# A six-layer local-attention stack: squares in halves, head scaling ahead of the score maximum, rotary tables scaled two steps earlier, and the value projection two units at a time in high and low parts

## The chip, the cores and the metric

The kernel runs on 1 core of one Trainium2 chip. The metric is the device time of one execution in microseconds. TensorE, VectorE, ScalarE and GpSimd each work through a queue of their own in program order; SyncE's queue issues the DMAs. They meet only at semaphores. In the rows below they are called PE, DVE, ACT, POOL and SPq.

## The reference, cut to what matters

The program is one decoder layer of three parts (a Mamba block with a mixture of experts, a cross attention, and a stack of six local-attention layers), each followed by a residual sum and a layer norm. All of the change that takes time lies in the third part, the stack. It runs over 2 batches of 512 tokens with 128 features, and each of its six layers does:

```python
def attn_layer(x, Wqkv, qs, ksc, Wo):          # 16 heads of 64, window 32
    q, k, v = split(x @ Wqkv, 3)
    q = l2norm(q) * qs
    k = l2norm(k) * ksc
    q = q * cos * scale + rotate_half(q) * sin * scale
    k = k * cos * inv   + rotate_half(k) * sin * inv
    sim = einsum(q, k of this window and the one before) * 8.0, masked
    out = softmax(sim) @ v
    return out @ Wo
for i in range(6):
    x = attn_layer(shift_tokens(x), ...) + x
    x = ffn_layer(shift_tokens(x), ...) + x     # layer norm, gated GELU, 341 wide
```

## The kernel before, in words

`build_stack` (line 1083) writes the stack out by hand as a software pipeline. A layer is a `turn`; a turn has 16 steps `t`, one for each *unit* (a pair of heads of one batch; units 0 to 7 belong to batch 0, units 8 to 15 to batch 1), so the stack has 96 units. In step `t` the five queues work on different units at once:

- TensorE: the scores of unit t+1 (`scores`, L1307), the projection of "head unit" h = t+4 into two PSUM banks (`project`, L1266 to L1270; q for even h, k for odd h, six matmuls of 512 columns in high and low fp32r parts), the transposes of the probabilities (L1319), the output projection of unit t-1 (L1341), the value projection of unit t+1 (`project_v`, L1290: four fp32 matmuls of 128 columns, which the trace shows as eight passes), the mask for the next scores, the sums of squares over a head (`head_norm`, L1278), and the values times the probabilities (L1331).
- ScalarE: the squares of the projection, both banks in one instruction (`square`, L1426), the exponential of the scores (L1489), the copies out of PSUM (L1457, L1466, L1450), and from the sum of squares the logarithm and the root (L1433, L1437).
- VectorE: the maximum of the scores of unit t+1 (L1610) and its subtraction (L1616); `normalise_heads` for head unit t+3 (L1556, writes `st_turned`); `rotate` for head unit t+4, which multiplies the projection by the sine and the cosine table (L1545, L1546); then the row sums (L1640) and their reciprocals (L1644).
- GpSimd: the sum of the two halves of squares (L1673); the two additions that end the rotation (L1677, L1678); the probabilities divided by their sum (L1685); in half of the steps the low part of a weight (L1662).
- SyncE: the DMAs that place the turned heads for the scores (four for a q unit, eight for a k unit), and two that shift the copied values (`shift_values`).

Head unit h is projected and rotated in step h-4 and scaled by `normalise_heads` in step h-3. That instruction waits for both of GpSimd's additions. `rotate` reads the PSUM banks, and the next `project` waits for both products, since there is one pair of banks. In the rows below the names of tiles that share memory are those of the first owner: `h` is the tile of squares, `x` the sine product or the copied output, `mo_w` the cosine product or the scaled probabilities.

In steps 0 to 3 and 8 to 11 of a turn the feed-forward layer of a batch runs in between, as `stage` 0 to 3. Stage 0: `residual1` on VectorE (L1564), then the mean on TensorE (L1345), `centre` on VectorE (L1580), the square on ScalarE (L1501) and the variance on TensorE (L1349), which stands ahead of the next step's scores. Stage 1 scales the centred rows and starts the gates, stage 2 multiplies gate and value on VectorE (`gated`), and the value projection there waits for that. Stage 3 ends with `down` on TensorE, `residual2` on VectorE (L1571), and where a new layer follows the high part of the stream on ScalarE (L1518), for which the next projection waits. In step 11 and step 12 of each turn but the last, `scale_table` (L1444, two instructions of 1024 elements) writes the rotary tables of the next layer; it stands at the step's end, ahead of L1518. In the first turn there is no feed-forward layer in steps 0 to 3, so stage 0 occurs 11 times beside steps 0 to 15, and once more behind them.

From step 7 to 14 VectorE writes one eighth of the next layer's q and k weights as fp32r (`high_weights`, L1536), and GpSimd its rest (`low_weights`, L1662).

## Time and profile before

| | us |
|---|---|
| median of 3 runs | 1337.75 (1335.63 to 1342.5) |
| the profiled execution | 1334.07 |
| its span | 1332.3 |
| TensorE busy in the span | 1143.7 (86%) |
| VectorE, ScalarE, GpSimd busy | 951.0, 834.3, 671.2 |

The span is what the profiler saw between the first and the last instruction; 1.8 us of the profiled execution's time lie around it. Busy time adds up instructions and says nothing of what waits for what. TensorE's granted clock was 0.99 to 1.00 of full speed (2.4 GHz) in every stretch of 130 or 140 us from 470 to 1160 us; the stack runs from before 437.75 us to about 1319 us. One turn, from the scores of step 8 at 632.83 us to those of the next turn's step 8 at 781.05 us, took 148.2 us.

### The profile page before, as it was taken

The numbers are of one execution on the slowest core, as the hardware profiler recorded it, in microseconds if no ns is written. First come the engines' busy times: TensorE is split into PE (matmuls) and PEld (weight loads), VectorE is DVE, ScalarE is ACT, GpSimd is POOL, SyncE is SP. The second block draws the span as 40 slices with busy tenths as digits, with TensorE's granted clock in tenths as the row PEclk, the third lists the DMA queues.
The fourth block names the chain that finished last, engine by engine and source line by source line (L and its number), as shares of the span: only waits on it lengthen the run. The fifth ranks groups of instructions, "written<-read, shape, count | busy, mean of one in ns | idle before, by whom it ended". The sixth has DMA issues, their size and how long they took to land. (4 is left out here: it accounts for less than half of the span.)

```text
span 1332.3 us, 25833 instructions
## 1 busy us (share of the span) xinstructions
PE 1143.7 (86%) x9541; PEld 716.3 (54%) x9636; DVE 951.0 (71%) x1207; ACT 834.3 (63%) x1260; POOL 671.2 (50%) x522
## 2 busy tenths in 40 slices
PE   7787879998656898998988998899989989899975
PEld 2222347776224665656555655656555655566541
DVE  2798957776646787877877787867877786877733
ACT  4553446665354667776776767676767667676834
POOL 1555524443326665755655465755555555645510
PEclk9888969999878999999999999999999999999987
DMA  3000035100203443445334442444333532434310
GB/s 108 1 0 0 1 49 198 48 24 1 95 1 79 128 111 77 108 103 132 80 92 105 116 111 72 110 115 121 78 92 102 134 96 69 108 91 110 87 46 16
DMA packets 75507, 107.08 MB, mean 80 GB/s; under 512 B 25347, under 2 KB 31938, under 8 KB 75002
## 3 DMA queue, kind: packets, MB, share of 16 engines
q1 hardware_dynamic: 75386, 105.47, 30.3%
q8 instruction: 76, 1.25, 0.4%
q14 instruction: 45, 0.37, 0.1%
HBM read 30.89 MB, written 0.59 MB: 24 GB/s over the span
## 5 line engine op out<-in xcount | busy, mean ns | idle before, releaser
L1673 POOL TENSOR_TENSOR st_sq_sum<-h 128x512 f32<-128x512 f32 x96 | 130.1, 1355 | 201.4 <-ACT h L1426 201.4
L1677 POOL TENSOR_TENSOR mo_w<-mo_w,x 128x512 f32<-128x512 f32 x96 | 122.3, 1274 | 154.0 <-DVE mo_w L1546 154.0
L1426 ACT ACTIVATE h<-banks 128x1024 f32<-128x1024 f32 x96 | 98.3, 1024 | 144.1 <-PE banks L1270 143.8
L1610 DVE TENSOR_REDUCE st_mx<-banks 128x8 f32<-128x512 f32 x96 | 66.4, 692 | 165.6 <-PE banks L1307 165.2
L1278 PE MATMUL banks<-st_sq_sum,head_ones 128*128 128x512 f32 x192 | 106.6, 637 | 47.9 <-POOL st_sq_sum L1673 46.6
L1556 DVE SCALAR_TENSOR_TENSOR st_turned<-st_rn,mo_w 128x1024 f32<-128x1024 f32 x96 | 124.3, 1295 | 5.9 <-POOL mo_w L1678 5.5
L1545 DVE TENSOR_TENSOR x<-banks,st_scaled 128x1024 f32<-128x1024 f32 x96 | 117.0, 1218 | 15.4 <-ACT h L1426 14.0
L1290 PEld LDWEIGHTS banks<-st_wv,stream 128*128 128x128 f32 x768 | 100.7, 192 | 49.7 <-issue 49.3
L1678 POOL TENSOR_TENSOR mo_w<-mo_w,x 128x512 f32<-128x512 f32 x96 | 122.5, 1276 | 0.0
L1307 PE MATMUL banks<-st_k_blocks,st_qT 128*32 128x128 f32 x3072 | 105.5, 279 | 16.9 <-DMA st_k_blocks<-st_turned 16.9
L1331 PEld LDWEIGHTS banks<-st_p_blocks,st_vs 128*64 128x64 f32 x1536 | 77.8, 137 | 74.2 <-issue 72.9
L1546 DVE TENSOR_TENSOR mo_w<-banks,st_scaled 128x1024 f32<-128x1024 f32 x96 | 116.4, 1213 | 0.0
L1457 ACT ACTIVATE st_p_blocks<-banks 64x512 f32<-64x512 f32 x192 | 112.3, 585 | 3.5 <-PE banks L1319 1.1
L430 POOL TENSOR_TENSOR ma_dbx<-ma_u,ma_b_rows 128x1024 f32<-128x1024 f32 x32 | 75.4, 2360 | 76.1 <-ACT ma_b_rows L288 51.9
L1266 PE MATMUL banks<-st_y_high,st_w_high 128*128 128x512 f32 x192 | 91.9, 479 | 21.2 <-issue 11.6
L1685 POOL TENSOR_TENSOR mo_w<-st_prob,st_ri 128x512 f32<-128x512 f32 x96 | 100.3, 1045 | 17.9 <-DVE st_ri L1644 17.9
L1290 PE MATMUL banks<-st_wv,stream 128*128 128x128 f32 x768 | 102.4, 277 | 0.8 <-issue 0.8
L1433 ACT ACTIVATE st_rn<-banks,fill 128x512 f32<-128x512 f32 x96 | 66.0, 688 | 58.9 <-PE banks L1278 58.9
L1341 PE MATMUL banks<-x,st_wo 128*128 128x512 f32 x192 | 101.7, 612 | 0.9 <-ACT x L1450 0.8
L1331 PE MATMUL banks<-st_p_blocks,st_vs 128*64 128x64 f32 x1536 | 99.4, 228 | 2.8 <-ACT st_p_blocks L1457 2.1
L1307 PEld LDWEIGHTS banks<-st_k_blocks,st_qT 128*32 128x32 f32 x3072 | 79.1, 111 | 41.5 <-DMA st_k_blocks<-st_turned 23.1
L1331 PE MATMUL banks<-st_p_blocks,st_vn 128*64 128x64 f32 x1536 | 94.8, 222 | 0.0
(230 smaller groups left out, 2629.2 us busy)
## 6 DMA issues: line engine op xcount, KB each, us to landing
st_qT<-st_turned SPq DMA_DIRECT2D x192, 128.0 KB, 2.4
st_k_blocks<-st_turned SPq DMA_DIRECT2D x384, 64.0 KB, 2.0
st_vs<-st_vn SPq DMA_DIRECT2D x96, 192.0 KB, 2.5
st_w_raw<-in_w_qk SPq DMA_DIRECT2D x12, 512.0 KB, 4.7
st_vs<-st_vn SPq DMA_DIRECT2D x96, 48.0 KB, 2.1
mo_w_all<-gate_rows SPq DMA_DIRECT2D x1, 3072.0 KB, 12.9
st_wv<-in_w_v SPq DMA_DIRECT2D x12, 256.0 KB, 3.0
st_wo<-in_wo SPq DMA_DIRECT2D x12, 256.0 KB, 3.1
```

The lines of the kernel that those rows point to most:

```text
L1278: mm(NORM_BANK, C["head_ones"], sq_sum[:], start=True, stop=True).then_inc(norm_done.sem, 1)
L1290: last = mm(V_BANK[:, rows], Y[:, b, rows], wv[:, pair, :], start=True, stop=True)
L1307: last = mm(SCORE_BANK[rows].rearrange("p (o h i k) -> p o h i k", o=2, h=2, i=2)[:, odd, :, i, :], qT[:, r, pair, t0:t0 + WIN], k_blocks[ ...
L1331: last = mm(TURN_BANK[rows, P * j:P * j + P].rearrange("p (h o q) -> p h o q", h=2, q=WIN)[:, :, odd, :], (vn if odd else vs)[:, r, j, row ...
L1341: mm(OUT_BANK[b], wo[:, pair, :], oT[:, n % 2, :], start=(pair == 0), stop=(pair == 7)).then_inc(wo_step.sem, 1)
L1457: A(p_blocks[rows, r, half, :], TURN_BANK[rows, :], ACT.Copy).then_inc(pt_copied.sem, 1)
L1545: v.tensor_tensor(sin_part[:], QK_BANKS, scaled[:, which, 1], ALU.mult).then_inc(product_done.sem, 1)
L1546: v.tensor_tensor(cos_part[:, which], QK_BANKS, scaled[:, which, 0], ALU.mult).then_inc(product_done.sem, 1)
L1556: v.scalar_tensor_tensor(turned[:, h % 4], rn[:, h % 2, :].unsqueeze(1).to_broadcast([P, 2, SEQ]), 1e12, cos_part[:, which], ALU.min, ALU. ...
L1673: nc.gpsimd.tensor_tensor(sq_sum[:], sq[:, 0, :], sq[:, 1, :], ALU.add).then_inc(sq_summed.sem, 1)
L1677: nc.gpsimd.tensor_tensor(cos_part[:, which, 0, :], cos_part[:, which, 0, :], sin_part[:, 1, :], ALU.subtract).then_inc(add_done.sem, 1)
L1678: nc.gpsimd.tensor_tensor(cos_part[:, which, 1, :], cos_part[:, which, 1, :], sin_part[:, 0, :], ALU.add).then_inc(add_done.sem, 1)
```

## The change

It has four parts, all in `build_stack`:

1. `square` writes two instructions of 512 elements, each behind its own half of the projection; `project` counts `qk_done` after each half.
2. `normalise_heads(t + 3)` moves on VectorE's queue from behind the score's maximum, subtraction and `residual1` to the very start of the step.
3. `scale_table` moves on ScalarE's queue from the end of steps 11 and 12 to their start.
4. The value projection works on two units' columns at once: 256 columns of weights and two of the four row tiles in each step, as three fp32r matmuls (high by high, high by low, low by high) for each tile. It and the copy run one step ahead (unit t+2); the shifting DMAs are issued every other step with twice the bytes. The weights of V get a high part on VectorE and a low part on GpSimd, four more of each per layer, in steps 8, 10, 12 and 14.

To make room, `gate`, `act` and `xn` move into tiles that are free by then (`cr_onehot`, `cr_line` and `cr_bias` in the rows of the new order).

```diff
 def square(s, h):
-            ac.wait_ge(*qk_done.at(s.turn, h + 1))
             if sq_summed.any(s.turn, h):
                 ac.wait_ge(*sq_summed.at(s.turn, h))
-            A(sq[:], QK_BANKS, ACT.Square).then_inc(sq_done.sem, 1)
+            for part in range(2):
+                ac.wait_ge(*qk_done.at(s.turn, 2 * h + part + 1))
+                A(sq[:, part, :], ps[:, part, :], ACT.Square).then_inc(sq_done.sem, 1)
...
 # ScalarE, body
+                if t in (11, 12) and not s.last:
+                    ac.wait_ge(*product_done.at(s.turn, 2 * (t + 4)))
+                    scale_table(s, t - 11, 1)
                 if stage == 1:
...
-                if t in (11, 12) and not s.last:
-                    ac.wait_ge(*product_done.at(s.turn, 2 * (t + 4)))
-                    scale_table(s, t - 11, 1)
                 if s.resplit(job, stage):
...
 # VectorE, body
                 n = t + 1
+                if t >= -3 and s.unit(t + 3):
+                    normalise_heads(s, t + 3)
                 if t >= -1 and s.unit(n):
...
                 if stage == 0:
                     residual1(s, job)
-                if t >= -3 and s.unit(t + 3):
-                    normalise_heads(s, t + 3)
...
 # VectorE, high_weights
             v.tensor_copy(w_high[:, i, :], w_raw[:, i, :]).then_inc(w_high_done.sem, 1)
+            if i % 2 == 1:
+                g = i // 2
+                dv.wait_ge(*places.wv_in.at(s.turn, 16 * ahead + 16))
+                if ahead:
+                    dv.wait_ge(*v_done.at(s.turn, 10 + 2 * g))
+                v.tensor_copy(wv_high[:, g, :], wv_raw[:, g, :]).then_inc(w_high_done.sem, 1)
...
 # TensorE, project_v
-            pe.wait_ge(*wv_in[pair // 4].at(s.turn, 16 * (n // 16) + 16))
-            for tile in range(4):
-                rows = slice(P * tile, P * tile + P)
-                last = mm(V_BANK[:, rows], Y[:, b, rows], wv[:, pair, :], start=True, stop=True)
+            if n % 16 < 8 and half == 0:
+                pe.wait_ge(*w_split.at(s.turn, SPLITS * (n // 16) + v_split(g)))
+            if n % 8 == 0:
+                pe.wait_ge(*y_low_done.at(s.turn, n // 8 + 1))
+            for i in range(2):
+                rows = slice(P * (2 * half + i), P * (2 * half + i) + P)
+                out = V_BANK[:, 2 * P * i:2 * P * i + 2 * P]
+                mm(out, y_high[:, b, rows], wv_high[:, g, :], start=True, stop=False)
+                mm(out, y_high[:, b, rows], wv_low[:, g, :], start=False, stop=False)
+                last = mm(out, y_low[:, b, rows], wv_high[:, g, :], start=False, stop=True)
...
-                if t >= -1 and s.unit(t + 1):
-                    project_v(s, t + 1, job, stage)
+                if t >= -2 and s.unit(t + 2):
+                    project_v(s, t + 2, job, stage)
```

How the order moves on VectorE, around a step without feed-forward work and one of stage 0 (step 0 of the second turn). Before:

```order
L1610 TENSOR_REDUCE st_mx<-banks 128x8
L1616 TENSOR_TENSOR st_prob<-banks,st_mx 128x512
L1564 TENSOR_TENSOR stream<-banks,stream 64x512 x2
L1556 SCALAR_TENSOR_TENSOR st_turned<-st_rn,mo_w 128x1024
L1580 TENSOR_TENSOR st_dx<-stream,banks 128x512
L1545 TENSOR_TENSOR x<-banks,st_scaled 128x1024
L1546 TENSOR_TENSOR mo_w<-banks,st_scaled 128x1024
L1640 TENSOR_REDUCE st_rs<-st_prob 128x8
```

The same place now, behind the reciprocal of the step before:

```order
L1574 SCALAR_TENSOR_TENSOR st_turned<-st_rn,mo_w 128x1024
L1630 TENSOR_REDUCE st_mx<-banks 128x8
L1636 TENSOR_TENSOR st_prob<-banks,st_mx 128x512
L1582 TENSOR_TENSOR stream<-banks,stream 64x512 x2
L1598 TENSOR_TENSOR st_dx<-stream,banks 128x512
L1563 TENSOR_TENSOR x<-banks,st_scaled 128x1024
L1564 TENSOR_TENSOR mo_w<-banks,st_scaled 128x1024
L1658 TENSOR_REDUCE st_rs<-st_prob 128x8
```

The rows are one step of stage 0; a regular step reads the same without the residual (64x512 x2) and without `st_dx`. The head scaling went from the third place to the first; maximum, subtraction and residual now stand behind it, and nothing is left between residual and centring.

On ScalarE, from the table load that ends step 10 to the stream's high part that ends step 11. Before:

```order
L1511 ACT_TABLE_LOAD
L1426 ACTIVATE h<-banks 128x1024
L1489 ACTIVATE st_prob<-st_prob 128x512
L1457 ACTIVATE st_p_blocks<-banks 64x512 x2
L1466 ACTIVATE st_vn<-banks 128x512
L1433 ACTIVATE st_rn<-banks,fill 128x512
L1437 ACTIVATE st_rn<-st_rn,fill 128x512
L1450 ACTIVATE x<-banks 128x512
L1444 ACTIVATE st_scaled<-st_table,st_rope_scale 128x2x512 x2
L1518 ACTIVATE st_y_high<-stream 128x512
```

Now:

```order
L1526 ACT_TABLE_LOAD
L1455 ACTIVATE st_scaled<-st_table,st_rope_scale 128x2x512 x2
L1437 ACTIVATE h<-banks 128x512 x2
L1504 ACTIVATE st_prob<-st_prob 128x512
L1468 ACTIVATE st_p_blocks<-banks 64x512 x2
L1478 ACTIVATE st_vn<-banks 128x512
L1444 ACTIVATE st_rn<-banks,fill 128x512
L1448 ACTIVATE st_rn<-st_rn,fill 128x512
L1461 ACTIVATE x<-banks 128x512
L1530 ACTIVATE st_y_high<-stream 128x512
```

The scaled tables went from ahead of the stream's high part to ahead of the squares, which are two instructions now; between them the order is the same.

## Rows read from the trace of the kernel before

**Rows 1.** The page: the span, and each engine's busy time.

```profile
span 1332.3 us, 25833 instructions
PE 1143.7 (86%) x9541; PEld 716.3 (54%) x9636; DVE 951.0 (71%) x1207; ACT 834.3 (63%) x1260; POOL 671.2 (50%) x522
```

**Rows 2.** The page, costliest groups: busy, mean ns of one | idle before, releaser.

```profile
L1278 PE MATMUL banks<-st_sq_sum,head_ones 128*128 128x512 f32 x192 | 106.6, 637 | 47.9 <-POOL st_sq_sum L1673 46.6
...
L1307 PE MATMUL banks<-st_k_blocks,st_qT 128*32 128x128 f32 x3072 | 105.5, 279 | 16.9 <-DMA st_k_blocks<-st_turned 16.9
```

**Rows 3.** Timeline, 700 to 712 us, a regular step: start, duration, engine, line, [idle before].

```profile
702.33 1.08 PE L1307 MATMUL banks<-st_k_blocks,st_qT 128*32 128x128 f32 x32 [1.50 <-DMA st_k_blocks<-st_turned]
...
703.48 0.69 DVE L1610 TENSOR_REDUCE st_mx<-banks 128x8 f32<-128x512 f32 x1 [2.95 <-PE banks L1307]
...
703.92 0.40 PE L1270 MATMUL banks<-st_y_low,st_w_high 128*128 128x512 f32 x1
...
704.16 0.40 PE L1266 MATMUL banks<-st_y_high,st_w_high 128*128 128x512 f32 x1
...
704.81 1.22 DVE L1556 SCALAR_TENSOR_TENSOR st_turned<-st_rn,mo_w 128x1024 f32<-128x1024 f32 x1
...
705.05 1.02 ACT L1426 ACTIVATE h<-banks 128x1024 f32<-128x1024 f32 x1 [3.34 <-PE banks L1270]
...
706.11 1.22 DVE L1545 TENSOR_TENSOR x<-banks,st_scaled 128x1024 f32<-128x1024 f32 x1
706.15 1.05 PE L1290 MATMUL banks<-st_wv,stream 128*128 128x128 f32 x8
...
707.25 1.22 DVE L1546 TENSOR_TENSOR mo_w<-banks,st_scaled 128x1024 f32<-128x1024 f32 x1
...
707.49 1.12 PE L1278 MATMUL banks<-st_sq_sum,head_ones 128*128 128x512 f32 x2 [0.28 <-POOL st_sq_sum L1673]
...
708.55 1.27 POOL L1677 TENSOR_TENSOR mo_w<-mo_w,x 128x512 f32<-128x512 f32 x1 [1.11 <-DVE mo_w L1546]
...
709.63 1.08 PE L1307 MATMUL banks<-st_k_blocks,st_qT 128*32 128x128 f32 x32
...
711.02 1.04 POOL L1685 TENSOR_TENSOR mo_w<-st_prob,st_ri 128x512 f32<-128x512 f32 x1
```

**Rows 4.** Timeline, 545 to 549 us, VectorE and GpSimd.

```profile
546.08 2.05 DVE L1556 SCALAR_TENSOR_TENSOR st_turned<-st_rn,mo_w 128x1024 f32<-128x1024 f32 x1 [0.29 <-POOL mo_w L1678]
...
546.00 1.04 POOL L1685 TENSOR_TENSOR mo_w<-st_prob,st_ri 128x512 f32<-128x512 f32 x1
```

**Rows 5.** Timeline, 712 to 721 us, a step of stage 0.

```profile
712.11 1.40 DVE L1564 TENSOR_TENSOR stream<-banks,stream 64x512 f32<-64x512 f32 x2
...
713.56 1.12 PE L1345 MATMUL banks<-stream,mean_ones 128*128 128x512 f32 x2
...
715.95 1.12 PE L1278 MATMUL banks<-st_sq_sum,head_ones 128*128 128x512 f32 x2 [0.37 <-POOL st_sq_sum L1673]
...
718.46 0.61 ACT L1501 ACTIVATE st_dsq<-st_dx 128x512 f32<-128x512 f32 x1
...
720.18 1.08 PE L1307 MATMUL banks<-st_k_blocks,st_qT 128*32 128x128 f32 x32
```

**Rows 6.** Timeline, 667 to 678 us, step 11 of a turn and what follows.

```profile
667.33 1.02 ACT L1426 ACTIVATE h<-banks 128x1024 f32<-128x1024 f32 x1
...
673.50 1.53 DVE L1571 SCALAR_TENSOR_TENSOR stream<-banks,st_ffn_param,stream 64x512 f32<-64x512 f32 x2 [1.93 <-PE banks L1376]
...
675.08 2.17 ACT L1444 ACTIVATE st_scaled<-st_table,st_rope_scale 128x1024 f32<-128x1024 f32 x2
...
677.16 0.62 ACT L1518 ACTIVATE st_y_high<-stream 128x512 fp32r<-128x512 f32 x1
```

**Rows 7.** Groups by line and form: the casts of q and k weights on VectorE.

```profile
L1536 DVE CAST st_w_high<-st_w_raw 128x256 fp32r<-128x256 f32 x48 | 33.5, 699 | 0.0
```

**Rows 8.** Timeline, 659 us, stage 2: the weight loads of the value projection.

```profile
659.20 0.97 PEld L1290 LDWEIGHTS banks<-st_wv,stream 128*128 128x128 f32 x8 [0.97 <-issue]
```

More of the change, by code:

```diff
@@ L1280, in project_v @@
         def project_v(s, n, job, stage):
-            b, pair = n // 8 % 2, n % 8
+            b, g, half = n // 8 % 2, n % 8 // 2, n % 2
             if v_copied.any(s.turn, n):
@@ L1329, in values @@
                         rows = slice(64 * head, 64 * head + 64)
+                        cols = slice(P * r + 64 * head, P * r + 64 * head + 64)
                         at = P * (2 * odd + head) + WIN * j
                         last = mm(TURN_BANK[rows, P * j:P * j + P].rearrange("p (h o q) -> p h o q", h=2, q=WIN)[:, :, odd, :],
-                                  (vn if odd else vs)[:, r, j, rows], p_blocks[:, r, :, at:at + WIN],
+                                  (vn if odd else vs)[:, q, j, cols], p_blocks[:, r, :, at:at + WIN],
                                   start=True, stop=True)
@@ L1356, in up_gate @@
             if j == 1:
-                pe.wait_ge(*v_copied.at(s.turn, min(t + 2, UNITS) if s.last else t + 2))
+                pe.wait_ge(*v_copied.at(s.turn, min(t + 3, UNITS) if s.last else t + 3))
             if j == 2:
@@ L1367, in up_value @@
             else:
-                pe.wait_ge(*v_copied.at(s.turn, min(t + 1, UNITS) if s.last else t + 1))
+                pe.wait_ge(*v_copied.at(s.turn, min(t + 2, UNITS) if s.last else t + 2))
                 pe.wait_ge(*act_done.at(s.turn, 3 * job + 2))
@@ L1596, in gated @@
                 dv.wait_ge(*w2_step.at(s.turn, 3 * job))
[L1597 removed]
+            v.scalar_tensor_tensor(act[0:rows, j, :], (OUT_BANK[job % 2] if j == 0 else V_BANK)[0:rows, :], ffn_param[0:rows, 2 + j:3 + j], gate[j % 2][0:rows, :],
                                    ALU.add, ALU.mult).then_inc(act_done.sem, 1)
@@ L1802, in program @@
         with ExitStack() as part:
-            spare = (x[:], h1[:], x1[:], weights.all[:].rearrange("p e g c -> p (e g) c"))
+            spare = (x[:], h1[:], x1[:], weights.all[:].rearrange("p e g c -> p (e g) c"), cross.place["bias"][:].rearrange("p t h k -> p t (h k)"),
+                     (cross.onehot[:, 0:SEQ], cross.line[:, 0:SEQ]))
             build_stack(nc, part, Y, stack, spare, d, C)
```

110 lines of the change are left out of this document (57 added, 53 removed).

## The prediction

> **What bounds the kernel now.** I read the page first. TensorE is busy 86% of the span and nothing else is over 71% [rows 1], which looks like a TensorE bound, but the list of groups shows what stands ahead of its instructions: 47.9 us of idle time before the head sums (they wait for GpSimd's sum of squares) and 16.9 us before the scores (they wait for the DMAs that place k) [rows 2]. These two waits are what the change is aimed at, so the question is what takes their place. For that I went to the timeline of one regular step [rows 3]. It runs from the scores at 702.33 us to those at 709.63 us, 7.30 us, and two chains hardly leave each other room in it. One is TensorE's queue, with 0.28 us of waiting. The other goes through three engines: the second product of the rotation ends at 707.25 + 1.22 = 708.47; GpSimd adds from 708.55 on and is free for the probabilities at 711.02, so the additions end about 2.55 us behind the products; the head scaling needs them. Before the change that scaling (704.81) comes behind the maximum (703.48) and the subtraction, when the additions are long done. Take from this: the additions end 1.4 us *behind* the start of the scores (711.02 against 709.63), while the maximum could start 1.15 us behind it (703.48 against 702.33).
>
> **Part 2, the order on VectorE.** I begin with this because it decides. VectorE now stands at the head scaling until the additions are done, and maximum, subtraction and the next rotation stand behind it. That closes a loop with nothing parallel in it: rotation, additions, scaling, maximum, subtraction, rotation. Its length from the rows: 2.55 to the end of the additions [rows 3], then the scaling starts 0.08 us behind GpSimd's probabilities [rows 4], maximum and subtraction take 1.33 (703.48 to 704.81), the rotation 2.36 (706.11 to 708.47) [rows 3]. The scaling itself has two prices in the trace: 1.22 alone [rows 3], and 2.05 in the one place where it had waited for the additions [rows 4]. There GpSimd's probabilities had started 0.08 us earlier, ran 1.04, and VectorE's instruction ended 1.22 - 0.13 behind them: it stood still until they were done. After the change this is the normal case, since GpSimd's probabilities follow the additions at once in its queue. So I take 2.05. Sum: 2.55 + 0.08 + 2.05 + 1.33 + 2.36 = 8.37; successive starts on VectorE overlap the end before by up to 0.1, so 8.3 us. With 1.22 it is 7.5 us.
>
> The Trainium skill (SBUF — State Buffer, "two separate sides") says that a VectorE instruction with two SBUF inputs and a GpSimd one that reads SBUF exclude each other on a shared port pair, and that whichever starts first has it to its end. The trace agrees in the row with 2.05. By that rule alone the 0.08 us decide: were the scaling first, the loop would be the 7.5 us one, and it is a rival below.
>
> Regular steps, without feed-forward work and not directly behind `residual2`, are 96 - 44 - 11 = 41. Each goes from 7.3 to 8.3: +41 us. The loop hides the DMA waits: the scaling of k ends earlier by more than the 1.50 us of the longest shown wait, so the 16.9 us go [rows 2, 3]. Net **+24**; with 7.5 us steps it would be 8 - 17 = -9.
>
> Stage 0, 11 times. The mean needs `residual1`, which needs the loop's first half. From the end of the products: 2.63 + 2.05 + 1.33 = 6.0, residual 1.40, 0.05 to the mean: 7.46. From the mean to the head sums 2.39 less the 0.37 waited there, less 0.15 for the cheaper value projection: 1.87. Head sums to the centred square 2.51, that to the next scores 1.72 [rows 5]. Sum 13.56. Before: 708.47 to 720.18, 11.71 [rows 3, 5]. +1.85 x 11 = **+20**; with a scaling of 1.22, +1.0 x 11 = 11. The head scaling used to fill VectorE's wait for the mean; now it stands empty.
>
> **Part 1, squares in halves.** Two instructions of 512 (0.61 for such a square [rows 5]) for one of 1.02 [rows 3]; the first is hidden under the second half of the projection, so the rotation could start some 0.4 us earlier. That removes head-sum waits only where TensorE is the bound. In the 41 regular steps the loop of part 2 does not contain the squares, so nothing is gained. Upper end if it did: the whole 47.9 us [rows 2]. In stages 1 and 2 some of it stays.
>
> **Part 3, tables early.** In step 11 the squares start at 667.33 with no idle time shown: ScalarE comes from a table load and is late already [rows 6]. Putting 2.17 us of tables there delays squares, sum of squares, head sums, `down` and `residual2` by 2.17 + 0.17. What comes back: the high part of the stream started at 677.16 and `residual2` had ended at 675.03 [rows 6], so up to 2.1 us. But behind it VectorE has to scale, find the maximum, subtract, cast twice and rotate before the next products, so I count 1.1 back, between 0 and 2.1. +1.25 x 5 turns = **+6** (ends +1 and +12).
>
> **Part 4, V in parts.** TensorE: six passes of 256 columns. A pass of 512 fp32r columns follows the last after 0.24 (703.92, 704.16), so 0.12 x 6 = 0.72 against 1.05 for the eight now [rows 3]; with a tail I take 0.15 saved, bounds 0 and 0.33. Over 96 units that could be 14 us, up to 32, if TensorE were the bound; I credit it only in stage 0, above, since elsewhere it turns into waiting. VectorE: 20 more casts of 0.70 [rows 7], 14 us if all lay in the loop, none if all fell into idle time; most of their steps are stage steps, so **+3**. Their low parts lie on GpSimd behind the probabilities, in time in which it waits. Fewer, larger shift DMAs free SyncE's queue, which is no longer what is waited for: nothing.
>
> **Stages 1 and 2.** Stage 2's value projection waits already for VectorE's gate products (0.97 us of idle time before its weights [rows 8]), and these stand behind a scaling that is 0.83 longer: +9 over 11 times. Against it stand the head-sum waits of stage 1, some 0.4 each, and 0.15 for V: -6. **+3**, ends -10 and +15.
>
> **Sum:** 24 + 20 + 6 + 3 + 3 = +56 on the profiled execution's 1334.1 us: **1390 us**. The median of the three runs stands 3.7 us above that execution, which is inside their spread.
>
> **The rivals.**
> *A, no stretch* (0.14). The scaling starts ahead of GpSimd's probabilities, or the pair at [rows 4] is a special case. For it: nearly all scalings before took 1.22, and 0.08 us is little. Against: both wait for the same additions, one of them in the queue right behind. Then -9 + 11 + 6 + 3 - 3 = +8: 1342 us, within 0.5% or just outside.
> *B, TensorE stays the bound* (0.10), the faster side. The place is the top of the step: if the additions end before the scores do, the scaling runs in time in which VectorE is idle (2.95 us ahead of the maximum at 703.48 [rows 3]) and delays nothing. It decides from the point where additions plus scaling (2.55 + 1.3 behind the products) end by 1.15 us behind the scores' start; now they would end 2.7 behind it. Squares in halves give back 0.4 of the missing 1.5, stretched DMA waits in odd steps the rest at times. Price: most of 47.9 and 16.9, and 14 for V, less 20 in stages 0 and the tables: about -45, 1290 us.
> *C, it costs more* (0.12). The low parts of V's weights and q's and k's (half of the steps) push GpSimd's sum of squares behind the maximum, casts then stand behind that sum as the scaling stands behind the probabilities, and stages 1 and 2 lose 1 to 2 us each: +20 more, 1410 us.
> That the change doesn't do what it says is excluded by the order of the new kernel's queues: the scaling does stand first.
>
> **How the numbers follow.** A measurement of this kernel tells about 0.5% (6.7 us) from no change. The forecast has 0.64, C 0.12, A 0.14, B 0.10. Slower by over 0.5%: the forecast, C and a third of A, 0.81. Within 0.5%: most of A, 0.09. Faster: B, 0.10. The range goes from below A (1342 less some 12 us of V that TensorE does give back) to C: 1330 to 1408, leaving out B and half of C.
>
> **What would show it.** Right: the idle time of VectorE moves from the maximum to the head scaling and names GpSimd's L1678 of before as its releaser; the mean duration of the scaling goes from near 1.22 to near 2; regular steps take 8.3 us and are even, without DMA waits; stage 0 grows by about 2 us; the transposes of the probabilities or the mean gain idle time on TensorE. Step by step wrong: a scaling of 1.22 us (A); regular steps under 7.3 us with the head sums' wait gone (B); squares of step 11 not later (part 3). If TensorE's idle time in the stack shrinks in total, the theory falls.

## The result and the profile after

| | before | after |
|---|---|---|
| median, 4 runs each on the same chip | 1336.69 us | 1402.14 us (1397.64 to 1406.66) |
| ratio, 95% interval | | 1.0483 (1.0448 to 1.0518) |
| the profiled execution | 1334.07 | 1398.13 |
| its span | 1332.3 | 1395.4 |

The change costs 65 us, 4.8%. The forecast was 1390 us, with a range of 1330 to 1408.

The page of the changed kernel, first its span and busy times, then the groups that answer to [rows 2] and the group of the head scaling:

```profile
span 1395.4 us, 25510 instructions
...
PE 1156.6 (83%) x9444; PEld 702.3 (50%) x9444; DVE 1009.8 (72%) x1231; ACT 851.8 (61%) x1356; POOL 707.7 (51%) x546
...
L1574 DVE SCALAR_TENSOR_TENSOR st_turned<-st_rn,mo_w 128x1024 f32<-128x1024 f32 x96 | 184.1, 1917 | 157.8 <-POOL mo_w L1700 149.0
...
L1281 PE MATMUL banks<-st_sq_sum,head_ones 128*128 128x512 f32 x192 | 110.3, 658 | 38.4 <-POOL st_sq_sum L1695 37.8
...
L1316 PE MATMUL banks<-st_k_blocks,st_qT 128*32 128x128 f32 x3072 | 105.5, 279 | 5.6 <-DMA st_k_blocks<-st_turned 5.6
```

TensorE's share fell from 86% to 83%. Of the two waits at which the change aims, the one for k's DMAs shrank, from 16.9 to 5.6 us. The head sums' seems to have fallen too, from 47.9 to 38.4 us, but the 47.9 us of [rows 2] are not all idle time. The mask's matmul stands right ahead of the head sums in TensorE's queue, and 95 of its 96 records are missing from the trace of the kernel before, so that its time reads as idle there. The trace of b3 below, whose edit leaves these instructions alone, has all of them. First the mask's matmuls before, then those of b3 and b3's head sums:

```profile
L1296 PE MATMUL banks<-mask,ident x1: 379/379/379, 417.1 to 417.1; 128*128 128x512 bf16 x1
...
L1296 PE MATMUL banks<-mask,ident x96: 379/379/650, 411.6 to 1273.6; 128*128 128x512 bf16 x96
...
L1278 PE MATMUL banks<-st_sq_sum,head_ones 128*128 128x512 f32 x192 | 108.8, 649 | 29.8 <-POOL st_sq_sum L1673 27.2
```

Against 29.8 us the head sums of the changed kernel wait longer, not shorter. With the mask left out of both traces it is 48.1 us before and 64.3 after. So 11 us of waits for DMAs are gone, and against them stand 158 us in which VectorE waits ahead of the head scaling, and a scaling that takes 1917 ns on average. Before, it took 1295 ns on average over the same 96. VectorE's wait costs time only where TensorE waits for VectorE in turn. Where that is, the waits list of the stack shows (engine, line, what it waited for: us in total, times, longest):

```profile
DVE st_turned L1574 <- POOL mo_w L1700: 131.1, 73, 1.8
...
PE banks L1355 <- DVE stream L1582: 28.2, 12, 2.6
...
PE banks L1281 <- POOL st_sq_sum L1695: 24.1, 31, 2.2
...
PE banks L1328 <- POOL mo_w L1707: 18.4, 25, 1.4
...
PE banks L1341 <- ACT st_p_blocks L1468: 14.7, 24, 1.9
...
PE banks L1297 <- DVE cr_bias L1615: 13.0, 17, 2.1
```

TensorE's waits are now spread over the whole step: for the residual ahead of the mean, for GpSimd's probabilities ahead of their transposes, for the copied probabilities, for the gates. No single one of them looks like the cause. I read them as places where TensorE meets a loop on the other engines that has become longer than its own work; the runs below test that.

**A regular step after the change.** The timeline from one step's scores to the next's, to be read beside [rows 3]:

```profile
643.48 1.08 PE L1316 MATMUL banks<-st_k_blocks,st_qT 128*32 128x128 f32 x32
...
644.07 1.29 POOL L1700 TENSOR_TENSOR mo_w<-mo_w,x 128x512 f32<-128x512 f32 x1
...
645.32 1.04 POOL L1707 TENSOR_TENSOR mo_w<-st_prob,st_ri 128x512 f32<-128x512 f32 x1
645.39 2.05 DVE L1574 SCALAR_TENSOR_TENSOR st_turned<-st_rn,mo_w 128x1024 f32<-128x1024 f32 x1 [1.80 <-POOL mo_w L1700]
...
647.36 0.68 DVE L1630 TENSOR_REDUCE st_mx<-banks 128x8 f32<-128x512 f32 x1
...
648.88 1.22 DVE L1563 TENSOR_TENSOR x<-banks,st_scaled 128x1024 f32<-128x1024 f32 x1
...
650.01 1.22 DVE L1564 TENSOR_TENSOR mo_w<-banks,st_scaled 128x1024 f32<-128x1024 f32 x1
...
651.31 1.28 POOL L1699 TENSOR_TENSOR mo_w<-mo_w,x 128x512 f32<-128x512 f32 x1 [2.73 <-DVE mo_w L1564]
...
651.75 1.08 PE L1316 MATMUL banks<-st_k_blocks,st_qT 128*32 128x128 f32 x32
```

651.75 - 643.48 = 8.27 us; the forecast was 8.3. The scaling waits 1.80 us, starts 0.07 us behind GpSimd's probabilities, stands still for as long as these run, and takes 2.05 us, as in [rows 4]. The maximum follows at 647.36, although its scores were there since about 644.6.

**A step of stage 0**, which answers to [rows 5]:

```profile
657.13 1.40 DVE L1582 TENSOR_TENSOR stream<-banks,stream 64x512 f32<-64x512 f32 x2
...
658.59 1.13 PE L1355 MATMUL banks<-stream,mean_ones 128*128 128x512 f32 x2 [2.56 <-DVE stream L1582]
...
659.75 0.69 DVE L1598 TENSOR_TENSOR st_dx<-stream,banks 128x512 f32<-128x512 f32 x1 [0.69 <-PE banks L1355]
...
660.50 1.02 PE L1281 MATMUL banks<-st_sq_sum,head_ones 128*128 128x512 f32 x2
...
662.91 0.61 ACT L1516 ACTIVATE st_dsq<-st_dx 128x512 f32<-128x512 f32 x1
...
664.63 0.65 PE L1316 MATMUL banks<-st_k_blocks,st_qT 128*32 128x128 f32 x16
```

From 651.75 to 664.63 it is 12.88 us (10.55 before). TensorE stands for 2.56 us in front of the mean, and VectorE for 0.69 us behind it with nothing to do.

**Step 11**, which answers to [rows 6]:

```profile
688.96 1.28 ACT L1526 ACT_TABLE_LOAD   x1
...
690.25 2.19 ACT L1455 ACTIVATE st_scaled<-st_table,st_rope_scale 128x1024 f32<-128x1024 f32 x2
...
692.35 1.06 ACT L1437 ACTIVATE h<-banks 128x512 f32<-128x512 f32 x2
...
694.81 1.97 PE L1281 MATMUL banks<-st_sq_sum,head_ones 128*128 128x512 f32 x2 [2.19 <-POOL st_sq_sum L1695]
...
700.25 1.53 DVE L1589 SCALAR_TENSOR_TENSOR stream<-banks,st_ffn_param,stream 64x512 f32<-64x512 f32 x2 [3.62 <-PE banks L1386]
...
701.83 0.62 ACT L1530 ACTIVATE st_y_high<-stream 128x512 fp32r<-128x512 f32 x1
```

The tables stand ahead of the squares, and the head sums wait 2.19 us. (They have moved from the end of their step to its start, not by two steps as the title has it.) What comes next costs again: the two head sums take 1.97 us where they take 1.02 in the stage 0 step above. The table of windows over the same place (window, length, busy time and count of PE, PEld, DVE, ACT, POOL, then PEclk, DMA share, GB/s):

```profile
690.00:694.80 4.80, 2.23 (x11) 1.09 (x9) 2.65 (x5) 4.76 (x8) 1.65 (x2) 1.00 0.50 111
694.80:698.00 3.20, 3.19 (x4) 1.41 (x5) 1.79 (x3) 1.96 (x4) 2.12 (x2) 0.52 0.37 99
```

Behind the wait the granted clock is 0.52, all but the lower of TensorE's two levels (1.2 GHz), for 3.2 us. Step 11 went from 11.17 us to 14.7 to 15.0 in four turns. In the first turn the wait is the same, 2.18 us, but the clock stays at 1.00 behind it, and the step takes 13.3 us: 2.1 more, which is the wait alone. So the low clock adds 1.4 to 1.7 us where it comes, and it does not come behind every such wait. The longer wait of stage 0, 2.56 us, shows the same. The next three rows are the stretches behind the wait of step 11 in the first turn, behind that of step 8 in the first turn, and behind that of the stage 0 step above:

```profile
535.70:538.70 3.00, 3.00 (x7) 1.44 (x8) 1.78 (x3) 2.21 (x4) 1.94 (x2) 1.00 0.34 87
500.40:503.40 3.00, 3.00 (x10) 1.89 (x8) 1.64 (x3) 0.27 (x2) 0.00 (x0) 0.50 0.39 92
658.60:661.60 3.00, 3.00 (x15) 1.69 (x17) 2.31 (x5) 1.02 (x3) 0.00 (x0) 1.00 0.40 96
```

Step 8 of the first turn takes 14.51 us, the others up to the last turn 12.88. Two of the eleven stage 0 steps have the low clock. The kernel before has such stretches too: each of its five steps 12 with tables has a wait of 2.32 us ahead of the projection; in four of them (10.9 to 11.2 us) the clock falls, in the fifth (10.56) it does not. What decides whether the clock falls behind a wait of this length is open.

**Where the time went.** I took the distance from one step's scores to the next in both traces, from step 3 of the first turn to the last scores of the stack (before 839.2 us, after 899.5), and summed the differences by kind of step, in us:

| steps | number | difference |
|---|---|---|
| stage 0 (0 and 8) | 11 | +25.7 |
| stages 1 and 2 (1, 2, 9, 10) | 22 | +7.5 |
| 3 | 6 | 0.0 |
| stage 3, tables in all turns but the last (11) | 6 | +16.9 |
| 12 | 6 | -18.0 |
| 4 to 7 | 24 | +10.3 |
| 13 to 15 | 16 | +17.9 |
| sum | 91 | +60.3 |

The rest of the 63.1 us between the spans lies ahead of step 3 (+3.9) and behind the last scores (-1.1). The rows mix the parts of the change; which part a difference belongs to only the runs below can tell.

### The profile page after: what moved, and what is told of

Same layout as the page of the kernel before. It is cut to its first block and busy times, and to the rows that moved or that the text cites. A ratio compares the mean times of both kernels' runs of the same rounds, so it can differ in the third digit from the quotient of the medians.

```text
span 1395.4 us, 25510 instructions
## 1 busy us (share of the span) xinstructions
PE 1156.6 (83%) x9444; PEld 702.3 (50%) x9444; DVE 1009.8 (72%) x1231; ACT 851.8 (61%) x1356; POOL 707.7 (51%) x546
## 5 line engine op out<-in xcount | busy, mean ns | idle before, releaser
L1574 DVE SCALAR_TENSOR_TENSOR st_turned<-st_rn,mo_w 128x1024 f32<-128x1024 f32 x96 | 184.1, 1917 | 157.8 <-POOL mo_w L1700 149.0
L1437 ACT ACTIVATE h<-banks 128x512 f32<-128x512 f32 x192 | 111.6, 595 | 86.0 <-PE banks L1273 83.4
L1281 PE MATMUL banks<-st_sq_sum,head_ones 128*128 128x512 f32 x192 | 110.3, 658 | 38.4 <-POOL st_sq_sum L1695 37.8
L1504 ACT ACTIVATE st_prob<-st_prob 128x512 f32<-128x512 f32 x96 | 60.5, 630 | 110.2 <-DVE st_prob L1636 110.2
L1341 PEld LDWEIGHTS banks<-st_p_blocks,st_vs 128*64 128x64 f32 x1536 | 81.7, 138 | 91.1 <-issue 88.4
L1297 PE MATMUL banks<-st_wv_high,st_y_high 128*128 128x256 f32 x192 | 85.6, 446 | 15.9 <-DVE cr_bias L1615 13.0
L1316 PEld LDWEIGHTS banks<-st_k_blocks,st_qT 128*32 128x32 f32 x3072 | 79.2, 111 | 29.8 <-issue 17.4
L370 DVE TENSOR_TENSOR_SCAN ma_state<-banks,ma_dbx 128x512 f32<-128x512 f32 x64 | 76.1, 1212 | 16.3 <-ACT banks L298 13.8
## 6 DMA issues: line engine op xcount, KB each, us to landing
mo_w_all<-gate_rows SPq DMA_DIRECT2D x1, 3072.0 KB, 12.8
```

What stands on the lines that cost most here:

```text
L1281: mm(NORM_BANK, C["head_ones"], sq_sum[:], start=True, stop=True).then_inc(norm_done.sem, 1)
L1316: last = mm(SCORE_BANK[rows].rearrange("p (o h i k) -> p o h i k", o=2, h=2, i=2)[:, odd, :, i, :], qT[:, r, pair, t0:t0 + WIN], k_blocks[ ...
L1341: last = mm(TURN_BANK[rows, P * j:P * j + P].rearrange("p (h o q) -> p h o q", h=2, q=WIN)[:, :, odd, :], (vn if odd else vs)[:, q, j, col ...
L1437: A(sq[:, part, :], ps[:, part, :], ACT.Square).then_inc(sq_done.sem, 1)
L1574: v.scalar_tensor_tensor(turned[:, h % 4], rn[:, h % 2, :].unsqueeze(1).to_broadcast([P, 2, SEQ]), 1e12, cos_part[:, which], ALU.min, ALU. ...
```

## The experiments

My theory was the forecast's: the scaling ahead of the maximum closes a loop (rotation, additions, scaling, maximum, subtraction), and GpSimd's probabilities stretch the scaling to 2.05 us in it. The main rival after the result was that the other parts cost more than I had said, the tables and V in parts above all. The ratios below are to the kernel before on the same chip, whose median was 1336.5 us beside a1, a2, a3 and b1, 1336.4 us beside a4, b2, b3 and b4, and 1334.2 us beside a6, a7, d1 and d2.

**a1: the changed kernel with the scaling at its old place.**

```diff
 # VectorE, body
-                if t >= -3 and s.unit(t + 3):
-                    normalise_heads(s, t + 3)
                 if t >= -1 and s.unit(n):
...
                 if stage == 0:
                     residual1(s, job)
+                if t >= -3 and s.unit(t + 3):
+                    normalise_heads(s, t + 3)
```

> The changed kernel with the head scaling back behind the maximum, the subtraction and the residual; squares in halves, early tables and V in parts stay. Theory (the loop through the head scaling is the cause): some 50 us of the 65 go, about 1350 us; regular steps about 7.2 us, the scaling mostly 1.22 us, stage 0 about 10.5 us. Rival (V in parts, with its casts on VectorE and low parts on GpSimd, is the cause): 1385 us or more.

Measured: 1355.89 us, ratio 1.0150 (1.0102 to 1.0198). 46 of the 65 us go. The other three parts together still cost 19 us. Its stage 0 is back at 10.6 to 11.0 us.

**b1: the kernel before with this part alone.** The edit of a1 the other way round, in the kernel before.

> The kernel before with only the head scaling moved to the start of the step. Theory: regular steps 8.3 us, scaling near 2.05 us, stage 0 near 12.5 us; about 1385 us, 45 to 55 more than before. Rival (V in parts or the tables are the cause): under 1355 us.

Measured: 1387.57 us, ratio 1.0399 (1.0363 to 1.0436). This one part costs 51 us. Its row on the page is that of the full change almost to the digit:

```profile
L1556 DVE SCALAR_TENSOR_TENSOR st_turned<-st_rn,mo_w 128x1024 f32<-128x1024 f32 x96 | 185.2, 1929 | 155.1 <-POOL mo_w L1678 152.4
```

Steps 6 and 7 of a turn mostly take 8.27 us in it, too, and the two waits of [rows 2] are 20.2 and 1.2 us, against 29.8 (with the mask's records, see above) and 16.9. So less waiting of the kind that was aimed at goes together with 51 us more.

Where they lie is a surprise. Summed as in the table above, the kernel is 47.2 us longer from step 3 on: 37.5 in stage 0, 5.8 in steps 4 to 7, 8.1 in steps 13 to 15, -3.0 in step 12 and -1.2 in stages 1 and 2 (steps 3 and 11 are unchanged). Four of the eleven stage 0 steps take 12.8 to 13.0 us; in the other seven (14.3 to 15.0 us) the granted clock falls to 0.50 for a stretch. Eleven of 91 steps carry most of the cost.

**a3: the stretch taken away, the order kept.** GpSimd's probabilities wait until the scaling is done, so that they cannot run beside it.

```diff
 # GpSimd, body
                     pool.wait_ge(*rec_done.at(s.turn, n + 1))
+                    if s.unit(h):
+                        pool.wait_ge(*rope_done.at(s.turn, h + 1))
```

> The changed kernel where GpSimd's scaled probabilities wait for the head scaling, so that the two never run at once. Theory (they exclude each other, and the one behind stands still): scaling 1.22 us, regular steps 7.5 us, about 35 us less, near 1365 us. Rival (2.05 us is what this instruction takes when it reads what was just written): scaling stays 2.05 us, and the time is the same or longer by the extra wait.

Measured: 1368.04 us, ratio 1.0240 (1.0204 to 1.0276), 34 us less than the full change. A regular step of it, from scores to scores, with the instructions of the hand-over:

```profile
643.85 1.29 POOL L1700 TENSOR_TENSOR mo_w<-mo_w,x 128x512 f32<-128x512 f32 x1
...
644.41 1.08 PE L1316 MATMUL banks<-st_k_blocks,st_qT 128*32 128x128 f32 x32
...
645.17 1.23 DVE L1574 SCALAR_TENSOR_TENSOR st_turned<-st_rn,mo_w 128x1024 f32<-128x1024 f32 x1 [1.79 <-POOL mo_w L1700]
...
646.53 1.04 POOL L1709 TENSOR_TENSOR mo_w<-st_prob,st_ri 128x512 f32<-128x512 f32 x1 [1.39 <-issue]
...
651.95 1.08 PE L1316 MATMUL banks<-st_k_blocks,st_qT 128*32 128x128 f32 x32
```

The scaling takes 1.23 us, all 96 of them 1225 ns on average. It still comes right behind the additions, so the rival (it is slow because it reads what was just written) is out. Steps 5 to 7 take 7.55 us (7.54 here) and stage 0 in step 8 takes 10.8. The wait of VectorE is the same 1.79 us as in the full change. So of the 46 us that the new order costs, some 34 go with the stretch, and 12 are left against a1. A wait that was *added* to GpSimd's queue made the kernel 34 us faster.

The 34 us are a net figure. From step 3's scores to the last ones the trace is 28.4 us shorter: 24.4 in stage 0, 8.0 in stages 1 and 2 and 7.0 in steps 4 to 7, while steps 12, 13 and 15 are 13.6 us longer. There TensorE waits up to 2.45 us for the probabilities, which now come later.

**a2: the tables back at the end of steps 11 and 12.**

```diff
 # ScalarE, body
-                if t in (11, 12) and not s.last:
-                    ac.wait_ge(*product_done.at(s.turn, 2 * (t + 4)))
-                    scale_table(s, t - 11, 1)
                 if stage == 1:
...
+                if t in (11, 12) and not s.last:
+                    ac.wait_ge(*product_done.at(s.turn, 2 * (t + 4)))
+                    scale_table(s, t - 11, 1)
                 if s.resplit(job, stage):
```

> The changed kernel with the rotary tables back at the end of steps 11 and 12. Theory: step 11 gets some 3.7 us shorter (2.2 of tables and the lower TensorE clock behind that wait), step 12 some 3 us longer; 2 to 7 us in all, about 1397 us. Rival (the tables explain a large part, since the lower clock spreads): 15 us or more.

Measured: 1394.67 us, ratio 1.0461 (1.0416 to 1.0507): 7.5 us less than the full change by the medians and 3 by the ratios, whose intervals overlap; from step 3 to the last scores it is 5.8 us in the traces. That is the order of what was expected. Step 11 takes 11.24 us instead of 14.7 to 15.0, step 12 takes about 11.0 instead of 7.83, and step 13 is 7.2 us shorter over the turns. Against these, stage 0 is 7.6 us longer: seven of its steps have the low clock, where the full change has two, so part of the net figure is the clock's. The early place is bad for steps 11 and 13 and good for step 12. That suggested a place between.

**b3: the kernel before with the tables ahead of the output copy of steps 11 and 12**, where ScalarE waits for TensorE.

```diff
 # ScalarE, body
+                if t in (11, 12) and not s.last:
+                    ac.wait_ge(*product_done.at(s.turn, 2 * (t + 4)))
+                    scale_table(s, t - 11, 1)
                 if t >= 0 and s.unit(t):
                     copy_out(s, t)
...
-                if t in (11, 12) and not s.last:
-                    ac.wait_ge(*product_done.at(s.turn, 2 * (t + 4)))
-                    scale_table(s, t - 11, 1)
                 if s.resplit(job, stage):
```

> The kernel before with the tables scaled in steps 11 and 12 just ahead of the copy of the output, where ScalarE sat idle for about 2.2 us. Theory: step 11 stays 11.2 us, step 12 goes from 11 to about 9 us since the high part of the stream no longer waits: 8 to 12 us less, about 1327 us. Rival (step 12 is bound by VectorE's and GpSimd's chain anyway, as the prediction counted it): 5 us or less.

Measured: 1324.71 us, ratio 0.9910 (0.9885 to 0.9935). ScalarE's timeline around the end of step 11, to be read beside [rows 6]:

```profile
672.93 2.17 ACT L1444 ACTIVATE st_scaled<-st_table,st_rope_scale 128x1024 f32<-128x1024 f32 x2
...
675.74 0.62 ACT L1518 ACTIVATE st_y_high<-stream 128x512 fp32r<-128x512 f32 x1
```

The tables run in time in which ScalarE was idle, and the high part starts 0.61 us behind the scores of step 12 (675.13) instead of 2.69 behind them (677.16 against 674.47). Step 11 keeps its 11.17 us, step 12 falls from 10.6 to 11.2 down to 8.5 to 9.5. The 12 us of this run are those that part 3 was after; the changed kernel's early place gives them back in steps 11 and 13. Part of the gain is the clock's: the stretches of low clock in step 12 are gone.

**b2: the kernel before with the squares in halves alone.** The edit is part 1 of the change.

> The kernel before with only the squares in halves. Theory (the squares lie on the chain projection, squares, rotation, additions, probabilities, transposes that shares the bound with TensorE in regular steps): regular steps 7.0 to 7.1 us instead of 7.3, the head sums' wait near nothing, 5 to 12 us less, about 1328 us. Rival (TensorE's own queue is the bound, or the longer DMA wait takes it back): under 4 us.

Measured: 1333.47 us (12 runs), ratio 0.9977 (0.9958 to 0.9996): 3 us, less than I expected. The head sums' group shows where to look:

```profile
L1279 PE MATMUL banks<-st_sq_sum,head_ones 128*128 128x512 f32 x192 | 107.1, 640 | 26.3 <-POOL st_sq_sum L1675 25.6
```

The page's 47.9 us before would make this a fall of 21.6 us, but this trace has the mask's 96 matmuls that the other lacks. Against b3's 29.8 us the fall is 3.5, and with the mask left out of both traces it is 8 (48.1 to 40.1). The time fell by 3. Summed over the stack, steps 1, 5, 7 and 14 are 5.7 us shorter; step 8 is 2.3 longer, because a scaling that now comes earlier meets a low part on GpSimd and takes 1.68 us in place of 1.22; and what steps 5 and 7 gain comes back in part in step 6, 0.8 us.

**b4: both**, squares in halves and tables ahead of the output copy.

> Both of these edits in the kernel before. The two act in different steps, so the gains should add up: about 1318 us. If they don't, they work on one and the same wait.

Measured: 1322.21 us, ratio 0.9891 (0.9868 to 0.9913). The gains of the two, 3 and 12 us, add up to the 14 of this run.

**a4: V in parts alone**, which is the changed kernel with parts 1 to 3 undone.

> The changed kernel with the three other parts undone: V two units at a time in high and low parts alone. Theory after the first runs (the low parts lie ahead of the sum of squares in GpSimd's queue, and the casts behind it on VectorE; larger loads collide with the heads' DMAs in the first layer): slower than before by 10 to 15 us, 1350 us, in steps 9, 13 and 15 and once in step 4 of the first layer; steps 5 to 7 no slower. Rival (the prediction's: 3 us on VectorE, less what TensorE gains): within 5 us of before.

Measured: 1349.44 us, ratio 1.0091 (1.0065 to 1.0118). V in parts costs 13 us by itself. TensorE's six passes are cheaper than the eight before, but a regular step still takes 7.30 us. The trace puts the cost in three places.

The first is the first layer. The load of V's weights, which the kernel before issues in two halves in steps 11 and 15, is one DMA of 512 KB in step 3 now, right behind two loads for q and k and ahead of the DMAs that place k. SyncE's issues and the scores that wait for them:

```profile
460.66 1.17 SPq L1059 DMA_DIRECT2D st_w_raw<-in_w_qk  x2
461.87 0.43 SPq L1062 DMA_DIRECT2D st_wv_raw<-in_w_v  x1
...
464.23 5.55 SPq L1214 DMA_DIRECT2D st_k_blocks<-st_turned  x8
...
472.38 1.94 PE L1315 MATMUL banks<-st_k_blocks,st_qT 128*32 128x128 f32 x32 [4.51 <-DMA st_k_blocks<-st_turned]
```

The scores wait 4.51 us and then take 1.94 us instead of 1.08; the granted clock is 0.50 from 471.5 to 478.3 us. Steps 4 and 5 of the first turn are 3.39 and 2.26 us longer than before, the second by the low clock. The second place is ahead of step 3: its scores stand at 449.1 to 453.3 us in the seven traces with V in parts, and at 444.2 to 449.0 in the seven without it. The means are 451 and 447, so some 4 us, between executions that differ by as much. From the stack's first scores to those of step 3 alone, the four with V in parts and the old order take 33.4 to 35.6 us and the six without V in parts and with that order 32.6 to 33.2, so about 2 of the 4 us are the stack's; the rest is not shown to be V's. The third is the other layers: step 9 waits 1.63 us for the sum of squares behind a low part (10.84 us, 9.98 before) and step 15 waits 1.15 us (8.5 to 9.6 us).

**a6: a4 with small parts of V in the later layers.** Of V's weights for layers 2 to 6 only 8 of 256 columns get a high and a low part; the instructions and their waits stay.

```diff
-                v.tensor_copy(wv_high[:, g, :], wv_raw[:, g, :]).then_inc(w_high_done.sem, 1)
+                w = 8 if ahead else 2 * P
+                v.tensor_copy(wv_high[:, g, 0:w], wv_raw[:, g, 0:w]).then_inc(w_high_done.sem, 1)
...
-                nc.gpsimd.tensor_tensor(wv_low[:, g, :], wv_raw[:, g, :], wv_high[:, g, :], ALU.subtract).then_inc(w_split.sem, 1)
+                w = 8 if ahead else 2 * P
+                nc.gpsimd.tensor_tensor(wv_low[:, g, 0:w], wv_raw[:, g, 0:w], wv_high[:, g, 0:w], ALU.subtract).then_inc(w_split.sem, 1)
```

> V two units at a time in high and low parts alone, where the parts of V's weights of the second to sixth layer are written for 8 of 256 columns only, so that those layers multiply old weights: instructions and waits stay, their length goes. Theory (the casts and low parts are what V in parts costs beside the load in the first layer): steps 9, 13 and 15 get back 1 to 1.3 us each, about 1341 us. Rival (the waits or TensorE's new passes cost it): 1347 us or more.

Measured: 1346.45 us, ratio 1.0080 (1.0054 to 1.0107). The median fell by 3 us, and by the ratios hardly at all. The profiled executions say more: from step 3's scores to the last ones a4 takes 850.3 us, a6 842.4, the kernel before 839.2. In that stretch the 8 us are there (step 9 back at 10.07 us alone is 3.8 of them), and outside of it the two executions differ by 2.6 us the other way. So the casts and low parts of the later layers cost something between 1.5 us (the ratios) and 8 us (the stretch). The later layers multiply old weights in this run; its instructions and waits are those of a4.

**a7: a4 with the load of V's weights in step 6 instead of step 3.**

```diff
 # SyncE, body
                         for half in range(2):
                             places.load_qk(sp, d, turn + 1, half)
-                        places.load_v(sp, d, turn + 1)
                         sp.wait_ge(*scaled_done.at(turn, 4))
                         places.load_scale(sp, d, turn + 1)
+                    if t == 6:
+                        places.load_v(sp, d, turn + 1)
```

> V two units at a time in high and low parts alone, with the load of V's weights in step 6 instead of step 3. Theory (in the first layer three loads of 512 KB stand right ahead of k's DMAs in step 4 and hold them up): step 4 of the first layer, 12 us, goes to 8.5, and the scores' wait of 4 us in step 5 to about 1; 3 to 5 us less, about 1345 us. Rival (the loads of q and k weights do it alone): no change.

Measured: 1350.98 us, ratio 1.0124 (1.0081 to 1.0168), no gain in the median. The trace has the gain that was expected at its place:

```profile
468.52 1.08 PE L1316 MATMUL banks<-st_k_blocks,st_qT 128*32 128x128 f32 x32 [2.11 <-DMA st_k_blocks<-st_turned]
```

2.11 us of wait for 4.51, and steps 4 and 5 together 3.6 us shorter; step 15 took 1.7 us of it back over the turns. Its runs spread over 15 us (1342.54 to 1358.05), so the median cannot settle 2 or 3 us. The wait itself does not depend on one execution: in the six traces with V's load in step 3 the same scores wait 3.7 to 4.9 us, in the seven without V in parts 1.13 at most. The load ahead of k's DMAs is shown as the cause of the longer wait, not as a share of the median.

**d1: scaling first, only where the additions are long done.** This is b4 with the new order in steps 4 and 12 alone. They come behind the feed-forward layer's last step, in which VectorE waits for `down`, so that the additions are ready.

```diff
 # VectorE, body, in b4
+                if s.unit(t + 3) and (t in (4, 12)):
+                    normalise_heads(s, t + 3)
                 if t >= -1 and s.unit(n):
...
-                if t >= -3 and s.unit(t + 3):
+                if t >= -3 and s.unit(t + 3) and not (t in (4, 12)):
                     normalise_heads(s, t + 3)
```

> Squares in halves and tables in ScalarE's gap, and the head scaling ahead of the maximum in steps 4 and 12 alone, where VectorE comes late from the feed-forward layer and the additions and the probabilities are long done. Theory: there the move closes no loop and meets nothing on GpSimd (scaling 1.22 us), VectorE's work until the rotation stays the same, and k's DMAs start 1.3 us earlier, so the waits for them in steps 5 and 13 go: 5 to 11 us less than the two edits alone, about 1314 us. Rival (the later maximum costs as much there): within 3 us of the two edits alone.

Measured: 1309.11 us, ratio 0.9803 (0.9782 to 0.9824), 2% under the kernel before and the fastest kernel of this study. Against b4, which ran on another chip, it is 12 us by the ratios and 13.6 in the stretch of the traces. Step 12 of it, with the scores that begin it and the next step:

```profile
672.25 1.08 PE L1308 MATMUL banks<-st_k_blocks,st_qT 128*32 128x128 f32 x32
...
674.13 1.22 DVE L1558 SCALAR_TENSOR_TENSOR st_turned<-st_rn,mo_w 128x1024 f32<-128x1024 f32 x1
...
675.38 0.69 DVE L1614 TENSOR_REDUCE st_mx<-banks 128x8 f32<-128x512 f32 x1
...
679.78 1.08 PE L1308 MATMUL banks<-st_k_blocks,st_qT 128*32 128x128 f32 x32
```

No wait ahead of the scaling, no stretch, and a step of 7.53 us. The gain was at or above the upper end of what I expected (5 to 11 us). Against b4, step 4 gives 7.2 us over the turns, step 12 another 8.6, and steps 13 and 5 give 3.0 and 2.3 back. The waits for k's DMAs at the end of steps 4 and 12, 0.54 to 3.25 us each in b4, are gone; their total on the page falls from 22.1 to 7.0 us, as the theory had it.

**d2: the same in steps 4, 6, 12 and 14**, two of which are regular steps.

```diff
-                if s.unit(t + 3) and (t in (4, 12)):
+                if s.unit(t + 3) and (t in (4, 6, 12, 14)):
```

> The same, and also in steps 6 and 14, in the middle of the regular steps. Theory: there the scaling waits for the additions again and takes 2.05 us; the rotation of that step comes 8.3 us behind the one before, but the DMA wait of the next step goes (0.4 to 1.7 us) and the steps between have slack: within 4 us of the kernel with steps 4 and 12 alone, more likely slower. Rival (it is the DMA wait that counts): 5 us less.

Measured: 1314.64 us, ratio 0.9858 (0.9841 to 0.9876), 5.5 us above d1. Step 6 takes 7.8 to 8.5 us with a scaling of 2.05, and step 15 behind the new step 14 takes 8.6 in place of 7.7. The order that wins in step 12 loses in steps 6 and 14: whether the additions are done decides.

Not tried: V in parts without the extra casts and low parts of the first layer, V in parts on top of d1, and another place for the low parts in GpSimd's queue.

## Why the prediction was right, point by point

**The loop of part 2** held to 0.03 us where nothing else interferes, in steps 5 to 7: 8.27 for 8.3, and 2.05 for the scaling. The choice between its two prices was the one that mattered, and a3 shows it: at 1.22 the same order gives steps of 7.55 (7.5 in the forecast) and 34 us less (the forecast's two sums, 1390 and 1342, differ by 48). The Trainium skill (SBUF — State Buffer, "two separate sides") has the one that starts first keep the shared port to its end. Here GpSimd starts 0.07 to 0.09 us earlier in every regular step from step 4 of the first turn on, and the scaling takes 2.05 us in each, which agrees.

**"Regular steps +41 us, less 16.9 of DMA waits" (+24).** The forecast counts 41 steps that belong to no stage and do not stand right behind `residual2`. With the order alone (b1) 39 of them, all but the last two, are 23.7 us longer, as forecast, but they are not even: steps 14 and 15 take 8.6 to 9.3 us, not 8.3. In the full change the same steps are 37.5 us longer. What comes on top belongs to other parts: V's load in steps 4 and 5 of the first turn (5.4), the early tables in step 13, which takes 9.8 to 10.0 us, and V's low parts in step 15.

**The steps right behind `residual2`** (4 and 12) are in the forecast's sum only with the 1.1 us that the tables give back. They are 9.5 us shorter in b1 and 24.1 in the full change, whose early tables shorten step 12. In them the scaling waits for nothing and takes 1.22 us, which d1 later made use of. This is a gain that the forecast did not see.

**"Stage 0, +1.85 x 11 = +20".** Measured +25.7: +1.7 in step 0 and +2.3 in step 8 where the clock stays up, and 3.4 and 4.0 in the first of each kind, where it falls. The forecast has no term for the clock. With the order alone it fell in seven of eleven such steps, and stage 0 cost 37.5 us.

**"Tables +6".** Step 11 was forecast at +2.34 each. In the one turn in which the clock stays up it is +2.1, in the other four 3.5 to 3.8. What comes back was mis-sized too: step 12 is some 3 us shorter, where I had "1.1 back". Step 13, which becomes longer, was not in the sum. Between these errors the net is small: 3 to 7.5 us by a2.

**"Stages 1 and 2, +3".** Measured +7.5, from +1.8 in step 10 down to -0.4 in step 1, inside the ends given. It is not the longer scaling alone: in b1 these stages are 1.2 us shorter.

**"V in parts: +3 on VectorE, low parts in time in which GpSimd waits, shift DMAs nothing".** This is the step that failed. V alone costs 13 us (a4). I had priced its instructions and not its load: that stands ahead of k's DMAs in the first layer and makes the scores wait 4.5 us. Nor did I follow the low part in step 9, behind which the head sums wait 1.6 us for the sum of squares. The credit for cheaper TensorE passes was worth nothing in a regular step, as said there: 7.30 us with them and without.

**"Part 1, nothing".** No run takes the halves out of the changed kernel, so this is not tested there; alone they give 3 us. The upper end, "the whole 47.9 us", was never there to be had: some 18 us of it are the mask's matmuls, by b3's 29.8.

The separate effects add up to about the whole: +51 for the order (b1), -3 for the halves (b2), +13 for V (a4) and +3 to +7.5 for the tables (the full change less a2) make +64 to +68 against +65 measured. The forecast's +56 came near it with errors on both sides: too little for V, stage 0 and the clock, and nothing for what steps 4 and 12 gain. The mechanism was right; that the sum is only 9 us off is in part luck.

Rival A fell with the 2.05 us, rival B with the waits behind the additions. TensorE's idle time, the span less its busy time, rose from 188.6 us to 238.8, though the mask's missing matmuls count as idle in the first. Rival C, "it costs more", had the right place for a part of it, the low parts; at 1.5 to 8 us (a6) they cost less than the 20 that it gave them.

## What to carry to other kernels

An instruction that waits for GpSimd's result should not run beside the next instruction of GpSimd's queue: read in the trace what that queue does in the 0.1 us behind the release, and if it touches SBUF too, let it wait (34 us here for one added wait). Before an instruction is moved ahead of others on its engine, compare when its inputs are ready with when those of the others are, and do so by kind of step: the same move gained some 12 us in steps 4 and 12 and cost 51 everywhere. Before a wait on the page is taken as the prize, compare the number of matmuls with the number of weight loads (x9541 and x9636 in [rows 1], x9636 twice in b2): where records are missing, the time of the missing instruction reads as a wait of the next one. And give a new wait on TensorE two prices, with and without the low clock behind it.

## What the runs showed of the hardware that I had not expected

- A wait of 2.2 us on TensorE was followed by 3.2 us at a granted clock of 0.52, in which two head sums took 1.97 us instead of 1.02. The same wait (2.18 us) was followed by a clock of 1.00 in another turn, and waits of 2.56 us by 0.50 in one turn and by 1.00 in four others. In steps 0, 8 and 11 of the changed kernel those with the low clock are 1.4 to 1.7 us longer than their like.
- Three loads of 512 KB, issued ahead of eight DMAs of 64 KB on the same queue, made the scores wait 4.5 us for those (3.7 to 4.9 in six traces); with two such loads it was 2.1 (a7) and, in the same place of the kernel before, 1.1.
- Between executions, what lies ahead of step 3 differs by some 4 us even where the code up to there is the same (445.2 us in the kernel before, 449.0 in b3). The stretch between two named instructions in the trace showed 8 us (a6) and 2.5 us (a7) that the medians of 4 to 6 runs did not.
